# A new timetable for the tails of a two-layer transformer kernel: consumers a slot behind producers, FFN output in two halves, PSUM banks shared by pairs of tiles

## The reference

```
x = x + attn0(layernorm(x)); x = x + ffn0(layernorm(x))
x = x + attn1(layernorm(x)); x = x + ffn1(layernorm(x))
```

## Time and profile before

| | |
|---|---|
| median of three runs | 359.61 us |
| profiled execution | 359.73 us, span of its instructions 358.0 us |
| busy of the span | PE 299.5 us (84%), DVE 258.4 (72%), ACT 220.4 (62%), POOL 156.4 (44%) |
| mean granted clock of TensorE | 0.955 |
| DMA | 59 GB/s in the mean, 20.2% of the engines' time |
| chain that ended last | PE 57%, DVE 14%, POOL 11%, ACT 9%, issue 7%, DMA 1% |

### The profile page before, as it was taken

The page is one execution under the profiler, slowest core; times in us unless marked ns, Lnnn a source line. Parts: engine busy times, 40 slices in busy tenths (PEclk is TensorE's granted clock), DMA queues, the critical chain, the costliest instruction groups (busy, mean ns, idle before and its releaser), DMA issues.

```text
span 358.0 us, 8359 instructions
## 1 busy us (share of the span) xinstructions
PE 299.5 (84%) x2832; PEld 210.3 (59%) x2832; DVE 258.4 (72%) x1009; ACT 220.4 (62%) x493; POOL 156.4 (44%) x367
## 2 busy tenths in 40 slices
PE   1761698696988989898989899999999999998754
PEld 1541465464756657575757576666667675764443
DVE  5784679788586767676676758768988989883433
ACT  5354267767576665666665666767776767677501
POOL 6263447867485757657574715220230303022020
PEclk9996659999999999999999999999999999999966
DMA  7567222314111122323000010101111110100001
GB/s 207 211 160 182 69 62 82 106 46 125 35 42 58 38 74 68 98 64 97 7 2 30 2 54 3 53 25 52 38 42 31 37 39 25 39 1 17 16 0 29
DMA packets 23034, 21.19 MB, mean 59 GB/s; under 512 B 2896, under 2 KB 20048, under 8 KB 22992
## 3 DMA queue, kind: packets, MB, share of 16 engines
q1 hardware_dynamic: 22992, 20.66, 20.2%
HBM read 13.18 MB, written 7.34 MB: 57 GB/s over the span
## 4 chain that ended last, share of the span: by engine, by line
PE 57%; DVE 14%; POOL 11%; ACT 9%; issue 7%; DMA 1%; POOLq 0%; ACTq 0%; SPq 0%; DVEq 0%
PE bank L860 14%; PE bank L834 5%; PE bank L892 4%; PE bank L901 4%; PE bank L935 4%; PE bank L815 3%; PE bank L838 3%; PE bank L779 3%; ACT PB L497 3%; POOL PB L390 3%; PE bank L816 3%; PE bank L927 3%; DVE JUNK L651 3%; PE bank L909 2%; DVE STAT L588 2%
## 5 line engine op out<-in xcount | busy, mean ns | idle before, releaser
L497 ACT ACTIVATE PB<-bank 128x384 f32<-128x384 f32 (+1 forms) x256 | 131.2, 547 | 35.3 <-PE bank L836 18.3
L654 DVE TENSOR_REDUCE NM<-bank 128x2 f32<-128x512 f32 x128 | 82.2, 682 | 16.2 <-PE bank L816 16.0
L834 PE MATMUL bank<-QS,KS 128*128 128x256 f16 x256 | 70.2, 275 | 7.5 <-ACT PB L497 6.2
L860 PE MATMUL bank<-PB,VP 128*32 128x256 f32 (+1 forms) x1024 | 61.7, 358 | 9.1 <-POOL PB L390 9.1
L649 DVE CUSTOM_DVE_ANT_0 JUNK<-bank,MSF 128x128 bf16<-128x128 f32 x128 | 36.3, 283 | 26.7 <-PE bank L813 26.4
L651 DVE CUSTOM_DVE_ANT_0 JUNK<-bank,MSF 128x256 bf16<-128x256 f32 x128 | 53.7, 419 | 0.0
L860 PEld LDWEIGHTS bank<-PB,VP 128*32 128x32 f32 x1024 | 26.7, 109 | 32.5 <-POOL PB L390 12.4
L390 POOL TENSOR_SCALAR_AFFINE_SELECT PB<-PB 128x512 f32<-128x512 f32 x64 | 41.6, 650 | 0.0
L415 POOL TENSOR_TENSOR xs<-xs,Y 128x256 f32<-128x256 f32 x8 | 5.8, 728 | 77.7 <-DVE Y L663 77.7
L834 PEld LDWEIGHTS bank<-QS,KS 128*128 128x128 f16 x256 | 24.5, 96 | 21.9 <-ACT PB L497 19.6
L815 PE MATMUL bank<-KS,QS 96*128 96x256 f16 x128 | 35.2, 275 | 0.8 <-DVE NM L654 0.8
(11 more groups left out here) (89 smaller groups left out, 619.4 us busy)
## 6 DMA issues: line engine op xcount, KB each, us to landing
scr<-PR SPq DMA_DIRECT2D x16, 256.0 KB, 2.8
QS<-scr SPq DMA_DIRECT2D x16, 128.0 KB, 2.6
QS<-scr SPq DMA_DIRECT2D x32, 64.0 KB, 2.9
KS<-scr SPq DMA_DIRECT2D x32, 64.0 KB, 2.9
KS<-scr SPq DMA_DIRECT2D x16, 128.0 KB, 3.0
scr<-PR SPq DMA_DIRECT2D x16, 128.0 KB, 1.9
out_x<-xs SPq DMA_DIRECT2D x8, 128.0 KB, 1.9
W<-in_w SPq DMA_DIRECT2D x1, 576.0 KB, 6.4
```

The costliest lines, as they stand in the source:

```text
L497: act.activation(PB[:, s % RING, 0:n], TB_[s % 2][:, 0:n], ACT.Exp).then_inc(s_e, 1)
L654: dve.tensor_reduce(m[:, s, 0:2], o[:, :].rearrange("q (n k) -> q n k", n=2), AX.X, ALU.max, negate=True).then_inc(s_mx, 1)
L834: pe.matmul(o[:, 0:S], k[:, 0:P], q[:, :], start=True, stop=True)
L860: ins = pe.matmul(o, v, pr, start=(g % 2 == 0 and kt == 0), stop=True, skip_group_check=True)
```

## The change

The `TAIL` table and all `if s == ...` lines of the tails go. In their place stands `STEP`, which gives every instruction group of a tail, on whichever engine, its own (phases later, slot), with `STEP_LAST0` for some steps of the first layer's batch 7, and `BANK` for the banks. `due` tells which batch has a step at slot s of phase i. In detail:

- Consumers stand at least a slot behind producers: oT0 at slot 4 and its normalisation at 5 (both were 3), zT 9, wo 10 with its add at 11, h0 at slot 1 and h1 at 5 of the second phase, the four relus singly at 2, 4, 6, 7, the add of f at 9, its statistics at 13 and norm2 at 14 (were 7 and 8), xT2 in the third phase at 2, Q and K singly at 12 and 13, V and the two parts of Q and K in the fourth phase. The tail of a first-layer batch is about a phase longer.
- The FFN output f is computed in two halves of its contraction, chunks 0 and 1 at slot 7 ("fa") and 2 and 3 at slot 8, into one accumulation.
- zT is written into the upper half of the bank that mr0 of the next phase uses, and V (v1) into the upper half of mr1's; one fill and one release serve both tiles.
- V is copied by ACT without its bias; POOL adds bv to x in the second-layer phase of the batch ("bv", slot 10), ahead of the residual add. The low part of Q and K moves from DVE to POOL ("lo1").
- POOL's norm subtracts the mean instead of adding the negated mean; the multiply L352 goes.
- M0, M1 = 9, 0; the last PV group of a phase comes at slot 2 of the next (was 1) and its copy on ACT at slot 3 (was 1). Spread of V on POOL at slot 8 (was 7).
- Second layer: oT1 4, xT3 13, gu0, gu1, gu2 at 1, 5, 9, all in bank 7 (were 3, 6, 12 in banks 7, 6, 7), dn in slot 12 of the second phase after (was slot 0 of the third). The loop ends a phase earlier. On SP the store of a batch's Q and K and of the output stand at other places.
- DVE's `held` memsets write different elements of HOLD.

The diff, cut to its core:

```diff
-M0, M1 = 10, 1
 EARLY = 4
 
 
-TAIL = (("oT0", 1, 3, 6), ("zT", 1, 7, 7), ("wo", 1, 10, 6), ("xT1", 1, 15, 7), ("h0", 2, 3, 7), ("h1", 2, 5, 7),
-        ("f", 2, 7, 6), ("xT2", 2, 12, 7), ("qk1", 2, 14, 6), ("v1", 3, 0, 6)), \
-       (("oT1", 1, 3, 6), ("xT3", 1, 10, 6), ("gu0", 2, 3, 7), ("gu1", 2, 6, 6), ("gu2", 2, 12, 7), ("dn", 3, 0, 6))
+STEP = ({"oT0": (1, 4), "norm_o": (1, 5), "zg": (1, 6), "z": (1, 7), "zT": (1, 9), "wo": (1, 10), "add_wo": (1, 11),
+         "norm1": (1, 12), "xT1": (1, 15), "h0": (2, 1), "relu0": (2, 2), "relu1": (2, 4), "xb": (2, 4), "h1": (2, 5),
+         "relu2": (2, 6), "relu3": (2, 7), "fa": (2, 7), "f": (2, 8), "add_f": (2, 9), "bn2": (2, 13), "norm2": (2, 14),
+         "xT2": (3, 2), "copy_xT2": (3, 3), "q1": (3, 12), "qk1": (3, 13), "copy_q1": (3, 13), "copy_k1": (3, 14),
+         "hi1": (4, 1), "lo1": (4, 2), "v1": (4, 0)},
+        {"bv": (0, 10), "oT1": (1, 4), "norm_o": (1, 5), "res": (1, 6), "bn3": (1, 7), "norm3": (1, 8), "xT3": (1, 13),
+         "lo3": (1, 14), "gu0": (2, 1), "hidden0": (2, 2), "gu1": (2, 5), "hidden1": (2, 6), "gu2": (2, 9), "hidden2": (2, 10),
+         "dn": (2, 12), "add_dn": (2, 13)})
+
+STEP_LAST0 = {"q1": (4, 10), "qk1": (4, 10), "copy_q1": (4, 10), "copy_k1": (4, 11), "hi1": (4, 13), "lo1": (4, 14)}
+
+BANK = {"oT0": 6, "wo": 7, "xT1": 7, "h0": 7, "h1": 7, "f": 6, "xT2": 6, "qk1": 6,
+        "oT1": 6, "xT3": 7, "gu0": 7, "gu1": 7, "gu2": 7, "dn": 6}
+M0, M1 = 9, 0
 
 
 STAGE_A = {4: dict(bn=-16, norm=-16, xT=-15, q=-13, k=-13, v=-10, rot_q=-12, rot_k=-11, sq_q=-11, sq_k=-10, hi=-9, lo=-7),
            5: dict(bn=-13, norm=-12, xT=-8, q=-6, k=-4, v=-3, rot_q=-5, rot_k=-3, sq_q=-4, sq_k=-2, hi=-1, lo=1),
            6: dict(bn=-4, norm=-3, xT=1, q=3, k=3, v=6, rot_q=4, rot_k=5, sq_q=5, sq_k=6, hi=7, lo=9),
-           7: dict(bn=8, norm=9, xT=16, q=19, k=22, v=28, rot_q=20, rot_k=23, sq_q=21, sq_k=24, hi=25, lo=27)}
-A_BANK = {4: (6, 6, 7, 6), 5: (6, 6, 7, 6), 6: (6, 6, 7, 6), 7: (6, 7, 6, 7)}
+           7: dict(bn=8, norm=9, xT=17, q=19, k=22, v=28, rot_q=20, rot_k=23, sq_q=21, sq_k=24, hi=26, lo=28)}
+A_BANK = {4: (6, 6, 7, 6), 5: (6, 6, 7, 6), 6: (6, 6, 7, 6), 7: (7, 7, 7, 6)}
...
+def slot_of(L, name, b):
+
+    off, s = STEP_LAST0[name] if (L, b) == (0, B - 1) and name in STEP_LAST0 else STEP[L][name]
+    return H * (when(L, b) + off) + s
+
+
+def due(L, name, i, s):
+
+    return [b for b in range(B) if slot_of(L, name, b) == H * i + s]
...
-        uses += [(H * (i - 1) + M0, 7, ("mr0", i)), (H * i + M1, 7, ("mr1", i))]
+        uses += [(H * (i - 1) + M0, 6 if phase(i - 3)[0] == 1 else 7, ("mr0", i)), (H * i + M1, 6, ("mr1", i))]
         L, b = ORDER[i]
-        uses += [(H * (i + off) + s, k, (name, b)) for name, off, s, k in TAIL[L]]
+        uses += [(slot_of(L, name, b), BANK[name], (name, b)) for name in BANK if name in STEP[L]]
...
-                L, b = phase(i - 3)
-                if L == 0:
+                L, b = phase(i - 4)
+                if L == 0 and b < B - 1:
                     store1(b)
-                if L == 1:
-                    store_out(b)
                 for (L, b), (j, place_) in LOADS.items():
...
                 if i + 1 < NPH:
                     load_max(i + 1, 0)
+                if i == when(0, B - 1) + 4:
+                    store1(B - 1)
+                L, b = phase(i - 2)
+                if L == 1:
+                    store_out(b)
...
-                pool.wait_ge(*emptied(f"v{L}", b))
+                if L == 0:
+                    pool.wait_ge(*emptied("v0", b))
+                else:
+                    pool.wait_ge(*emptied("mr1", when(0, b) + 4))
...
+                    for b in due(1, "bv", i, s):
+                        pool.wait_ge(s_xn[2], b + 1)
+                        pool.tensor_tensor(xt_(b), xt_(b), row(bv_row), ALU.add).then_inc(s_bv, 1)
+                    for b in due(0, "lo1", i, s):
+                        pool.wait_ge(s_hi1, b + 1)
+                        pool.tensor_tensor(PR1[b % 2][:, :, 1], QR1[b % 2][:, :, :], PR1[b % 2][:, :, 0],
+                                           ALU.subtract).then_inc(s_lo1, 1)
...
+            def relu(b, n):
+                m = psum(f"h{n // 2}", b)
+                if n % 2 == 0:
+                    act.wait_ge(*filled(f"h{n // 2}", b))
+                ins = act.activation(HR[:, n], m[:, (n % 2) * S:(n % 2 + 1) * S], ACT.Relu, bias=b1_col[:, n:n + 1])
+                if n % 2 == 1:
+                    ins.then_inc(*empties(f"h{n // 2}", b))
+
+            for i in range(-1, NPH + 2):
                 for s in range(H):
                     if 0 <= i < NPH:
                         exp(i, s)
+                    if s == 3 and 0 <= i - 1 < NPH:
                         evac_o(i - 1, 1)
+                    if s == 11 and 0 <= i < NPH:
+                        evac_o(i, 0)
+                    for b in due(0, "v1", i, s):
+                        act.wait_ge(*filled("mr1", i))
+                        act.copy(va_(b), upper(psum("mr1", i)))
                     if s == M1 and 0 <= i < NPH:
                         row_max(i, 1)
+                    for b in due(0, "zT", i, s):
+                        act.wait_ge(*filled("mr0", i + 1))
+                        act.copy(ZT[:, :], psum("mr0", i + 1)[:, S:2 * S])
                     if s == M0 and i + 1 < NPH:
                         row_max(i + 1, 0)
+                    for n in range(NI):
+                        for b in due(0, f"relu{n}", i, s):
+                            relu(b, n)
...
+                    for b in due(0, "copy_q1", i, s):
+                        act.wait_ge(*filled("qk1", b))
+                        if b >= 2:
+                            act.wait_ge(s_lo1, b - 1)
+                        act.activation(QR1[b % 2][:, 0], psum("qk1", b)[:, 0:S], ACT.Identity, bias=bqs_col, scale=QSCALE)
+                    for b in due(0, "copy_k1", i, s):
+                        act.activation(QR1[b % 2][:, 1], psum("qk1", b)[:, S:2 * S], ACT.Identity,
+                                       bias=bk_col).then_inc(*empties("qk1", b))
+                    for b in due(0, "hi1", i, s):
+                        if b >= 2:
+                            act.wait_ge(s_scr[1][b % 2], 32 * (b // 2))
+                        act.wait_ge(*emptied("qk1", b))
+                        act.copy(PR1[b % 2][:, :, 0], QR1[b % 2][:, :, :]).then_inc(s_hi1, 1)
...
-            def ffn0_out(c):
-                pe.wait_ge(*emptied("h1", c))
-                m = into("f", c)
-                for t in range(TPB):
-                    for n in range(NI):
+            def ffn0_out(c, h):
+
+                if h == 0:
+                    m = into("f", c)
+                else:
+                    pe.wait_ge(*emptied("h1", c))
+                    m = psum("f", c)
+                for t in range(TPB):
+                    for n in (2 * h, 2 * h + 1):
                         ins = pe.matmul(m[:, t * D:(t + 1) * D], HR[:, n, t * P:(t + 1) * P], wi2[:, n],
-                                        start=(n == 0), stop=(n == NI - 1))
-                ins.then_inc(*fills("f", c))
-
-            def project1(c):
+                                        start=(t == 0 and n == 0), stop=(n == NI - 1), skip_group_check=True)
+                if h == 1:
+                    ins.then_inc(*fills("f", c))
...
+                    if s == M1 and 0 <= i < NPH:
+                        m = into("mr1", i)
+                        for b in due(0, "v1", i, s):
+                            project1_v(b, m)
+                        max_rows(i, 1, m)
+                    if s == 2 and 0 <= i - 1 < NPH:
                         pv(i - 1, 3)
-                    if s == M1 and 0 <= i < NPH:
-                        max_rows(i, 1)
                     if s in PV and 0 <= i < NPH:
                         pv(i, PV.index(s))
                     if s == M0 and i + 1 < NPH:
-                        max_rows(i + 1, 0)
-                    if s == 0 and L3 == 0:
-                        project1_v(b3)
-                    if s == 0 and L3 == 1:
-                        ffn1_out(b3)
```

More of the change, by code:

```diff
@@ new lines, in _ @@
+                    for b in due(0, "zg", i, s):
+                        pool.wait_ge(*emptied("oT0", b))
+                        pool.tensor_tensor(halves(ZG), halves(Y), row(gate_row), ALU.mult).then_inc(s_zg, 1)
+                    for b in due(1, "res", i, s):
+                        pool.wait_ge(*emptied("oT1", b))
+                        pool.wait_ge(s_bv, b + 1)
+                        pool.tensor_tensor(xt_(b), xt_(b), halves(Y), ALU.add).then_inc(s_res, 1)
+                    for b in due(1, "norm3", i, s):
+                        norm(3, b)
@@ new lines, in _ @@
+                    for b in due(0, "norm1", i, s):
+                        norm(1, b)
+                    for b in due(0, "xb", i, s):
+                        pool.wait_ge(s_xn[1], b + 1)
```

(34 more changed lines are left out.)

243 lines of the change are left out of this document (85 added, 158 removed).

## The result

The changed kernel takes 376.29 us (median of 4 runs, 374.47 to 378.54) where the kernel before takes 359.68 on the same chip (median of 4): a ratio of 1.046, 95% interval 1.043 to 1.049. It is slower by 16.6 us, where 357.7 was forecast and the range ended at 363.5. The profiled execution took 374.47 us, its span is 372.7 (before: 358.0).

What follows compares the result with a forecast made beforehand. First-layer phases were taken as a cycle of waits with no engine full, second-layer ones as nearly filled by PE. Terms -7.25 (phases 1 to 9), +7.05 and -1.8 gave -2.0: 357.7 us from 359.73, range 352.5 to 363.5.

Steps and rivals of the forecast that it cites:

- the two normalisations 0.88: First-layer walk, POOL behind wo: two normalisations take 0.88 us, so xT1 can start at 14.95.
- signs that the prediction named for being wrong: Two observations: no wait of oT on bank 6, or a second-layer phase below 16.0 us.
- Phases 1 to 7: First-layer phases: -0.4 in 1, -1.3 in 2, -0.85 in 3 and 7, -0.94 each in 4 to 6.
- The start: Phase 0 and all ahead of it: no change, as what comes next waits for other things.
- The wait on bank 6: First-layer phases: PE waits 1.17 us before oT0, since xT2 holds bank 6 until its copy is through.
- Phases 8 and 9: Second-layer body with first-layer tails: 19.6 us (-0.25) and 18.5 us (-0.8).
- Phases 10 to 14: Second-layer phases get moved work and new waits of PE: +1.8 in 10, +2.65 in 11, +2.6 in 12 to 14.
- the second layer pays nothing: Rival for phases 10 to 14: the wait before oT1 only replaces existing waits; 353.3 us in all, chance 0.17.
- Phase 15 and the end: Last phase -1.1 us, the stretch behind the last PV group -0.7; together -1.8.
- lo1 on POOL: Low part of Q and K on POOL, taken as 1.46 us and hidden; unhidden up to 11.7 in all.
- This is where the change wins: First-layer slots 5 to 10: each consumer has one slot, so DVE's 1.6 us wait for the FFN output goes.
- POOL becomes the cycle: First-layer rival: POOL's row behind wo costs 8.55 instead of 7.65, phases stay near 19.2; 363.1 us, chance 0.22.

Runs made afterwards that it cites:

- b2: Kernel before with four forms of POOL's normalisation, one per norm (add or subtract, scalar from either tile); one execution, 363.67 us.
- a1: Changed kernel with POOL's normalisation as before put back (add the negated mean, with its extra multiply); 364.34 us, ratio 1.015.
- b1: Kernel before with only POOL's normalisation changed to subtract the mean, the negating multiply dropped; 366.12 us, ratio 1.020.
- a2: a1 with ACT's second O copy and copy of xT2 ahead of exp in slot 3; 353.63 us, ratio 0.986.
- a8: a1 with only the second O copy ahead of exp in slot 3, the copy of xT2 staying behind; one execution, 358.73 us.
- b3: Kernel before with DVE's add of the FFN output one slot later, at 8 instead of 7; 362.91 us, ratio 1.009.
- a5: a2 with the low part of Q and K (lo1) back on DVE in the same slot; 356.48 us, ratio 0.991.
- a6: a2 with both halves of the FFN output in slot 8; 353.86 us.

## Why the prediction was wrong

The step that failed is the one in the first-layer phases that says "the two normalisations 0.88". Rows 5 hold the form with add; the diff writes subtract, and that takes 1.58 for two on POOL (b2: 795 ns for 448 each). The step is in the walk twice, once by name and once inside "norm2 1.95", so POOL's row behind wo is 2 x 0.70 longer than it says. Measured from the end of wo to the last PV group, the row takes 9.1 where 7.65 was forecast. Against a1, which has the two small multiplies that the change drops, it is 1.16 a phase. The diff's operation was new, no row of before showed it on POOL, and it should have been bounded from both sides as lo1 was. Instead it was taken at its neighbour's price and a gain of 0.2 was booked for it.

This is the larger failure, but not the only one: with add (a1) the time is 364.34, still slower than before and above the range. What is left is spread over several terms, each too low by some tenths. Neither of the signs that the prediction named for being wrong came up: oT did wait for bank 6, and no second-layer phase with its full work fell below 16.0. Both signs stood for more gain than forecast, none for less.

- *Phases 1 to 7*: forecast -6.2, measured +4.80, a miss of 11.0. Of it 7.4 is subtract (after less a1: 0.60, 1.01, 1.15, 1.16, 1.16, 1.15, 1.16). The other 3.6 stays with a1, -2.59 instead of -6.2. About 0.3 a phase is TensorE's: from the PV group to the end of wo it takes 11.0 where 10.68 was forecast. I took 0.86 for each 256-column fp32 group and 0.44 for each of 128, but start to start they take 0.92 (h1), 0.47 (oT0) and 0.55 (wo), and each half of the FFN output 0.94 instead of 0.9. The kernel before shows unequal prices too: its h0, directly behind oT0, takes 0.86, its h1, behind scores, 0.94. The 15.4 of work was too low as well, and with it the 3.9 that a phase could gain: a1's phase of 18.94 has 2.7 of waits over 0.2 in it, by starts, and 16.2 besides. Another 0.3 is POOL's: a1 keeps the two small multiplies, which the forecast had taken out; after doesn't have them, and pays 1.4 for it.
- *The start*: forecast 0, measured +4.67. With add it is +0.70 in a1 and up to +2.9 in the other kernels with this start, so 1.7 to 4.0 hang on subtract (b1: 3.1). Four norms of POOL lie there, at 1.57 instead of 0.88: 2.8 if each is waited for. Which waits make it up isn't shown, and the clock of this stretch differs from run to run. "0, what comes next waits for other things" was argued, not walked.
- *The wait on bank 6*: forecast 1.17, measured 1.07, released by ACT's copy of XT as foretold. a2 and a8 show what it costs: 0.65 of 1.07 in a first-layer phase, 0.40 of it by the bank and 0.25 by the O copy.
- *Phases 8 and 9*: forecast -0.25 and -0.8; measured +0.62 and -0.83, with add +0.06 and -0.82. Phase 8 still has norms with their price.
- *Phases 10 to 14*: forecast +7.05, measured +7.74. The steps hold singly (0.51, 0.21, 0.97 for the forecast's 0.66, 0.23, 1.05). The rival "the second layer pays nothing" is refuted. That the O copy behind exp makes 0.73 of the 0.97 in each of phases 12 to 14 is shown by a8.
- *Phase 15 and the end*: forecast -1.8, measured -2.30; in a1 -0.86, since its end is 1.4 longer than after's. Phase 15 gives -1.05 of it, as forecast (-1.1). The rest, -1.25 for a forecast of -0.7, is no merit of the walk: the clock of this edge was 0.74 before and 0.84 after, and b3, which ends in the order of before, has a clock of 0.84 too and takes 20.91 there, after 20.94. At the same clock the new order of the end gains nothing in these two executions.
- *lo1 on POOL*: forecast at 1.46 hidden, measured 1.16 and hidden (a5). By the Trainium skill, "GPSIMD Engine Reference", "Engine selection", it was to be 1.36 for DVE's 0.68; the trace says 1.16, a factor of 1.7. That page's factor does not tell of the operation that decided: the two forms of `tensor_scalar` differ by 1.8 on one engine. The HELD of 0.70 is back at its 0.19 with DVE's two-input operation moved away, as the Trainium skill, "SBUF — State Buffer", "SBUF: two separate sides", has it.
- *"This is where the change wins"*, of the FFN output: half wrong. Its split brings nothing (a6), and one consumer moved behind its producer costs (b3). With add (a1), phases 1 to 7 win 2.6 of the 6.2 forecast, which the 7.7 of phases 10 to 14 outweigh.

The rival "POOL becomes the cycle" was right in its place, its order (norm1, cut, norm2, cut) and its effect, with a decision point of 19.1 that was passed by 1.0. It priced the way from wo to the last PV group at 8.55 where the forecast had 7.65; measured, from the end of wo, it is 9.1 in after (164.67 to 173.76) and 7.9 in a1. Its cause was another: it had been given the size of one more mask, not a norm of twice the length, and its total, 363.1, was 13 us short.

In sum: by medians 18.6 us lie between forecast and result. In the profiled spans it is 16.7 (372.7 for 356.0), of which 10.5 go with one operation (after less a1: start 4.0, phases 1 to 9 7.9, end -1.4, where a1 has the lower clock, 0.77 for 0.84) and 6.2 with the other terms: 3.6 in phases 1 to 7, 0.7 in the start, 0.3 in phases 8 and 9, 0.7 in phases 10 to 14, 0.9 in phase 15 and the end.
